# Up products of the first expert moved into the last attention pairs, and routed down products with token columns

## The reference

```python
# sixth block, T = 2048 tokens, 32 experts, top 8 (by groups), inner size 128
topk_idx, topk_w = _gate(x, gate_w, gate_bias)          # sigmoid scores, group-limited top 8
g = jnp.einsum('th,eih->eti', x, expert_gate)
u = jnp.einsum('th,eih->eti', x, expert_up)
outs = jnp.einsum('eti,ehi->eth', jax.nn.silu(g) * u, expert_down)
final = (gathered * topk_w[:, :, None]).sum(1)          # gathered: outs of the chosen experts
shared = _mlp(residuals, shared_gate, shared_up, shared_down)
x = x + final + shared
```

## Time and profile before

| | us |
|---|---|
| median of 3 runs (1290.94 to 1304.84) | 1292.93 |
| the profiled execution | 1292.72 |
| its span | 1290.9 |
| TensorE busy in the span | 1203.8 |
| VectorE, ScalarE, GpSimd busy | 805.8, 639.8, 559.0 |

### The profile page before, as it was taken

One profiled execution on the slowest core, in us unless ns is written; L12 is line 12 of the kernel. 1 busy time (PEld: TensorE's weight loads), 2 busy tenths in 40 slices (PEclk: granted clock), 3 DMA queues, 4 the chain that ended last, 5 costly groups with the idle time before them and its releaser, 6 DMA issues.

```text
span 1290.9 us, 31700 instructions
## 1 busy us (share of the span) xinstructions
PE 1203.8 (93%) x10556; PEld 985.2 (76%) x10564; DVE 805.8 (62%) x1769; ACT 639.8 (50%) x1389; POOL 559.0 (43%) x833
## 2 busy tenths in 40 slices
PE   6899999979997778998998999999999999999998
PEld 5677777757774446877776888888888888888887
DVE  4688888757776885648997776444444544444444
ACT  5766666634544886545555343433433433433333
POOL 2244444467774443548886423323323233233232
PEclk9899999989999998999998999999999999999999
DMA  8200000000000000210000133332333333333332
GB/s 283 60 18 16 16 16 8 2 1 2 0 0 33 1 0 16 68 42 2 0 1 1 44 117 116 106 110 100 114 114 110 109 133 107 114 114 103 110 99 77
DMA packets 34041, 80.13 MB, mean 62 GB/s; under 512 B 4416, under 2 KB 12096, under 8 KB 33984
## 3 DMA queue, kind: packets, MB, share of 16 engines
q1 hardware_dynamic: 32800, 78.09, 18.7%
q10 hardware_dynamic: 1184, 1.31, 0.3%
HBM read 77.03 MB, written 2.36 MB: 62 GB/s over the span
## 4 chain that ended last, share of the span: by engine, by line
PE 78%; DVE 8%; issue 5%; POOL 4%; ACT 4%; DMA 0%; DVEq 0%; POOLq 0%; ACTq 0%; SPq 0%
PE ps L2158 10%; PE ps L2160 10%; PE ps L2159 10%; PE ps L2179 5%; PE ps L2181 5%; PE ps L2180 5%; PE ps L421 4%; PE ps L968 3%; PE ps L436 3%; PE ps L409 3%; PE ps L959 2%; POOL Sm L1204 2%; PE ps L947 2%; PE ps L938 2%; PE ps L975 2%
## 5 line engine op out<-in xcount | busy, mean ns | idle before, releaser
L2417 POOL TENSOR_TENSOR sw<-sg,wb 128x512 f32<-128x512 f32 x136 | 176.9, 1301 | 392.2 <-ACT sg L2268 354.8
L2337 DVE TENSOR_TENSOR a<-sw,ps 128x512 f32<-128x512 f32 x136 | 93.5, 687 | 231.2 <-POOL sw L2417 230.9
L2273 ACT ACTIVATE ah<-a 128x512 fp32r<-128x512 f32 x136 | 86.1, 633 | 292.9 <-DVE a L2337 266.4
L2158 PE MATMUL ps<-Hh,wh 128*128 128x512 f32 x544 | 217.4, 400 | 0.3 <-issue 0.3
L2160 PE MATMUL ps<-Hh,wl 128*128 128x512 f32 x544 | 215.8, 397 | 0.0
L2159 PE MATMUL ps<-Hl,wh 128*128 128x512 f32 x544 | 215.8, 397 | 0.0
L2179 PE MATMUL ps<-wh,ah 128*128 128x256 f32 x544 | 153.8, 283 | 0.1
L2181 PE MATMUL ps<-wh,al 128*128 128x256 f32 x544 | 152.8, 281 | 0.0
L2180 PE MATMUL ps<-wl,ah 128*128 128x256 f32 x544 | 152.2, 280 | 0.0
L2341 DVE TENSOR_TENSOR al<-a,ah 128x512 fp32r<-128x512 f32 x136 | 96.3, 708 | 61.5 <-ACT ah L2273 58.1
L674 ACT ACTIVATE Pr<-ps,mx 128x256 f32<-128x256 f32 x256 | 103.9, 479 | 61.2 <-DVE mx L575 61.2
(11 more groups left out here) (227 smaller groups left out, 2443.1 us busy)
## 6 DMA issues: line engine op xcount, KB each, us to landing
wb<-token_weights SPq DMA_DIRECT2D x64, 512.0 KB, 3.6
raw<-in_ew SPq DMA_DIRECT2D x66, 384.0 KB, 3.0
cT<-in_ctxT SPq DMA_DIRECT2D x16, 256.0 KB, 2.7
cx<-in_ctxT SPq DMA_DIRECT2D x15, 256.0 KB, 2.7
X<-in_x SPq DMA_DIRECT2D x1, 1536.0 KB, 7.5
wqkv<-in_wqkv SPq DMA_DIRECT2D x2, 768.0 KB, 5.5
raw3g<-in_wg SPq DMA_DIRECT2D x1, 1024.0 KB, 5.4
raw3u<-in_wu SPq DMA_DIRECT2D x1, 1024.0 KB, 7.6
```

The source lines that it names most:

```text
L2158: eng.matmul(ps[:, bank, :], wh[:, u, w], HhT[:, c, cols], start=(c == 0), stop=False)
L2337: eng.tensor_tensor(a[:, tt, :], sw[:, tt, :], ps[:, UB[tt], :], ALU.mult).then_inc(m_a, 1)
L2417: eng.tensor_tensor(sw[:, tt, :], sg[:, tt, :], wb[:, u, tt * UT:(tt + 1) * UT], ALU.mult).then_inc(m_sw, 1)
```

## The change

1. The up products of n = 0, both halves, are issued inside body(15) of the attention: `first_up(0)` after scores(15,1), `first_up(1)` after rturn(12). The stretch by hand keeps the gate products of n = 0 alone, and those of half 1 now stand before pv(15,1).
2. The splits of the first two experts' gate and up weights move forward: first_high(0) in body(14) and first_high(1) in body(15) to just after turned(i-1,1), ahead of exps(i,0); first_low(0) in body(14) ahead of mask(14,1), first_low(1) after mask(15,1).
3. The router's first Sigmoid moves to body(15), ahead of exps(15,0). silu(0,0) moves ahead of turned(15,1).
4. From n = 4 on, down products have the down weights as stationary operand and stream 512 tokens of ah or al: 6 matmuls a half in place of 12. The sums are then transposed (256 columns x 512 tokens). `summed` copies them to SBUF (half by ScalarE, half by VectorE) and `turn_back` transposes them on TensorE in 8 transposes of 128 x 128 a half of 512 tokens, into the same banks, before `add`. This is done after n = 35 and after n = 67.
5. For n = 36 and 37 the order is written out: turn_back(0,0), gate_up(37) half 0, turn_back(0,1), down(36) half 0. The first add after n = 35 stays in VectorE's body(36), the second moves to body(37).

```diff
@@ attention, tensor body
                 scores(i, u, 1)
...
+            if closing(i) and not proj:
+                g["first_up"](eng, 0)
             if mid:
                 turn(i, u, 0)
...
                 g["route"]["turn"](eng, i - 3, v)
+            if closing(i) and not proj:
+                g["first_up"](eng, 1)
             if mid:
                 pv(i, u, 0)
@@ attention, vector body
+            elif not closing(i) and not proj:
+                g["first_low"](eng, 0)
             if tail:
                 normalise(i - 1, v)
...
                 mask(i, 1)
+            if closing(i) and not proj:
+                g["first_low"](eng, 1)
...
-            if not proj and isinstance(i, int) and i >= NPAIR - 2:
-                g["first_low"](eng, i - NPAIR + 2)
@@ attention, scalar body
                 turned(i - 1, 1)
+            if not proj and isinstance(i, int) and i >= NPAIR - 2:
+                g["first_high"](eng, i - NPAIR + 2)
+            if closing(i) and not proj:
+                g["route"]["scores"](eng, 0)
...
                 exps(i, 1)
-            if not proj and isinstance(i, int) and i >= NPAIR - 2:
-                g["first_high"](eng, i - NPAIR + 2)
@@ experts
+    def first_up(eng, tt):
+
+        if tt == 0:
+            eng.wait_ge(g["a_ve"], 8 * NPAIR)
+            eng.wait_ge(g["ln_hT"], g["lnt"][4] + NPAIR)
+        products(eng, 0, 0, tt, 0, 1)
@@ down
-            for j in range(4):
+            for m in range(0 if known(n, 4) else 2):
+                w = slice(512 + m * P, 512 + (m + 1) * P)
+                bank = ps[:, OB[tt] + m, :]
+                eng.matmul(bank, wh[:, u, w], ah[:, tt, :], start=first, stop=False)
+                eng.matmul(bank, wh[:, u, w], al[:, tt, :], start=False, stop=False)
+                ins = eng.matmul(bank, wl[:, u, w], ah[:, tt, :], start=False, stop=last)
+            for j in range(4 if known(n, 4) else 0):
...
+        def turn_back(s, tt):
+
+            eng.wait_ge(m_oa, 2 * s + tt + 1)
+            eng.wait_ge(m_od, 2 * s + tt + 1)
+            for j in range(4):
+                for m in range(2):
+                    at = DIM * (j % 2) + m * P
+                    ins = eng.transpose(ps[:, OB[tt] + j // 2, at:at + P], OT[:, tt, m, j * P:(j + 1) * P], ident[:, :])
+                if j % 2:
+                    ins.then_inc(m_tt, 1)
...
         vacated_front()
-        gate_up(0, 0, 0, 0)
+        half_up(0, 0, 0, 0, 0)
         turn(15, 1, 1)
         rturn(eng, 13, 1)
+        half_up(0, 0, 1, 0, 0)
         pv(15, 1, 1)
-        gate_up(0, 0, 1, 0)
...
-        for n in range(NE + 2, NE + 4):
-            step(n, n % 2, 1)
+        step(NE + 2, 0, 1)
+        turn_back(0, 0)
+        gate_up(NE + 3, 1, 0, 1)
+        turn_back(0, 1)
+        down(NE + 2, 0, 0)
+        gate_up(NE + 3, 1, 1, 1)
+        down(NE + 2, 0, 1)
...
+        for tt in range(2):
+            turn_back(1, tt)
@@ scalar
+        def summed(n, tt):
+
+            eng.wait_ge(m_d, given(m_d) + 2 * n - 2 + tt + 1)
+            eng.activation(OT[:, tt, 0, :], ps[:, OB[tt], :], ACT.Copy).then_inc(m_oa, 1)
...
-        route["scores"](eng, 0)
+        lg(eng, 12)
         eng.activation(warm[:, :], g["epsc"][:, :], ACT.Silu)
-        lg(eng, 12)
+        silu(0, 0)
         turned(15, 1)
-        silu(0, 0)
@@ vector, add and body
+                if group > 1 and j % 2 == 0:
+                    eng.wait_ge(m_tt, 4 * s + 2 * tt + j // 2 + 1)
...
+            if fixed == NE + 3:
+                add(NE + 2, 1)
...
+            if fixed == NE + 2:
+                summed(fixed, 1)
+                add(fixed, 0)
```

More of the change, by code:

```diff
@@ L2028, in experts @@
     sb, sem, ps, X, io, out = g["sb"], g["sem"], g["ps"], g["X"], g["io"], g["out"]
-    Hh, Hl, dram = g["Hh"], g["Hl"], g["wdram"]
+    Hh, Hl, dram, ident = g["Hh"], g["Hl"], g["wdram"], g["ident"]
     UT = 512
@@ L2048, in experts @@
     m_ah = sem(n + "ah", 3, "scalar"); m_al = sem(n + "al", 3, "vector")
-    m_y = sem(n + "y")
+    m_y = sem(n + "y"); m_oa = sem(n + "oa"); m_od = sem(n + "od"); m_tt = sem(n + "tt")
+    OT = g["self"]["Kbd"][:, :, :, :, :].rearrange("p u h b k -> p u h (b k)")
     g["m_out"] = m_out = sem(n + "out")
@@ L2090, in low_gu, with ready, products @@
                           ALU.subtract).then_inc(m_lg, 1)
+    def ready(eng, pairs):
+        eng.wait_ge(route["r_ht"], pairs)
+        eng.wait_ge(route["r_hl"], given(route["r_hl"]) + pairs)
+    def products(eng, n, u, tt, s, part):
+        if tt == 0:
+            eng.wait_ge(m_hg, weight(n) + 1)
+            eng.wait_ge(m_lg, given(m_lg) + weight(n) + 1)
+        if known(n, 3) and n != 1:
+            ready(eng, 8 * s + 4 * tt + 4)
+        cols = slice(2 * UT * s + UT * tt, 2 * UT * s + UT * (tt + 1))
+        bank, at, free, done = ((GB[tt], 0, m_sg, m_g), (UB[tt], 256, m_a, m_u))[part]
+        eng.wait_ge(free, given(free) + 2 * (n - 1) + tt + 1)
+        for c in range(HALF):
+            w = slice(at + c * P, at + (c + 1) * P)
+            eng.matmul(ps[:, bank, :], wh[:, u, w], HhT[:, c, cols], start=(c == 0), stop=False)
+            eng.matmul(ps[:, bank, :], wh[:, u, w], HlT[:, c, cols], start=False, stop=False)
+            ins = eng.matmul(ps[:, bank, :], wl[:, u, w], HhT[:, c, cols], start=False,
+                             stop=(c == 1))
+        ins.then_inc(done, 1)
+    def first_up(eng, tt):
+        if tt == 0:
+            eng.wait_ge(g["a_ve"], 8 * NPAIR)
+            eng.wait_ge(g["ln_hT"], g["lnt"][4] + NPAIR)
+        products(eng, 0, 0, tt, 0, 1)
     g["wb_ones"] = wb_ones
+    g["first_up"] = first_up
     g["first_high"] = lambda eng, c: high_gu(eng, c, c, 1)
@@ L2141, in tensor @@
     def tensor(eng):
-        def ready(pairs):
-            eng.wait_ge(route["r_ht"], pairs)
-            eng.wait_ge(route["r_hl"], given(route["r_hl"]) + pairs)
         def half_up(n, u, tt, s, part):
[L2148 to L2162, removed]
+            products(eng, n, u, tt, s, part)
         def gate_up(n, u, tt, s):
@@ L2187, in vacated_front @@
             eng.wait_ge(g["a_m"], 2 + 4 * NPAIR)
-            eng.wait_ge(g["a_ve"], 8 * NPAIR)
-            eng.wait_ge(g["ln_hT"], g["lnt"][4] + NPAIR)
         def vacated_back(tt):
@@ L2254, in tensor @@
             step(2 * j + NE + 5, 1, 1)
-        down(N - 1, 1, 0)
-        down(N - 1, 1, 1)
+        for tt in range(2):
+            down(N - 1, 1, tt)
+        for tt in range(2):
+            turn_back(1, tt)
     def scalar(eng):
@@ L2282, in body @@
             high_a(n, 0)
+            if isinstance(n, int) and n == NE + 2:
+                summed(n, 0)
             silu(n, 1)
@@ L2286, in body @@
             high_a(n, 1)
+            if isinstance(n, int) and n == NE + 2:
+                summed(n, 1)
             if isinstance(n, int) and n == NE + 3:
@@ L2324, in scalar @@
         from_sixth(eng, body)
+        summed(N, 0)
+        summed(N, 1)
     def vector(eng):
@@ L2342, in low_a, with summed @@
                               ALU.subtract).then_inc(m_al, 1)
+        def summed(n, tt):
+            eng.wait_ge(m_d, given(m_d) + 2 * n - 2 + tt + 1)
+            eng.tensor_copy(OT[:, tt, 1, :], ps[:, OB[tt] + 1, :]).then_inc(m_od, 1)
         def add(n, tt):
             group, s = GROUP.get(n, (3, 1))
-            eng.wait_ge(m_d, given(m_d) + 2 * n - 2 + tt + 1)
             if group > 1:
                 eng.wait_ge(m_y, 8 * group - 8)
+            else:
+                eng.wait_ge(m_d, given(m_d) + 2 * n - 2 + tt + 1)
             for j in range(4):
                 i = 8 * s + 4 * tt + j
+                if group > 1 and j % 2 == 0:
+                    eng.wait_ge(m_tt, 4 * s + 2 * tt + j // 2 + 1)
                 eng.tensor_tensor(X[:, i, :], ps[:, OB[tt] + j // 2, DIM * (j % 2):DIM * (j % 2 + 1)], X[:, i, :],
@@ L2361, in body @@
             low_a(n, 0)
-            if fixed in GROUP:
+            if fixed == 4:
                 add(fixed, 0)
+            if fixed == NE + 2:
+                summed(fixed, 0)
+            if fixed == NE + 3:
+                add(NE + 2, 1)
             if fixed in (5, 6, 7):
```

## The result

The changed kernel takes 1286.84 us (median of 19 runs, 1285.52 to 1293.9) against 1293.04 of the kernel before (19 runs). The ratio is 0.9957, 95% interval [0.9942, 0.9972], so 5.6 us faster (3.6 to 7.5). The forecast was 1292.5 with a range of 1288.0 to 1297.0. A gain of 0.4% is small, but the interval doesn't hold 1: with 19 runs of each kernel it can be told from none. The profiled execution of the changed kernel took 1291.0 us with a span of 1288.8.

The account below looks back on a forecast made before the run. TensorE, busy without a gap, was taken to bound the loop, and VectorE's chain to mul(1,0) the handover. Terms -2.6 + 2.1 + 2.1 - 1.8 = -0.2 us gave 1292.5 us, range 1288.0 to 1297.0.

Parts of the forecast that it names:

- Down products: Expert loop: 6 down matmuls of 512 columns for 12 of 256 save 2.6 us (1.3 to 3.8).
- 0.02 us less in each of 128 halves: Expert loop: a down half takes 1.40 us, 6 matmuls at the gate's 0.2333, instead of 1.42.
- Middle: Turning back after n = 35: transposes and a short wait add 2.1 us (1.8 to 2.7).
- The wait for adds behind low_a(37,0): In the middle: TensorE waits about 0.2 us for VectorE's moved adds, 0.6 if GpSimd slows VectorE.
- End: After the last product: a copy and all eight adds on VectorE make the end 2.1 us later (2.0 to 2.4).
- Handover: From attention to experts: four moves together bring VectorE's mul(1,0) 1.8 us earlier (-3.6 to 0).
- +0.35: Handover: Sigmoid and table loads ahead of exps(15,0) cancel the earlier mask's gain and delay it by 0.35 us.
- the lower clock from 698, as now: Handover: TensorE's clock still falls at 698, ending near 705 rather than 708.4; assumed for the -1.8 us.
- rival 1: Handover: the fill holds the clock up, front -3.6, sum -2.0, giving 1290.7 us; chance 0.20.
- The table switch of 2.66 us: ScalarE at the handover: by the skill, exps(15,0) would come 2.7 us later; the prediction used the trace instead.
- Sum: Whole kernel: loop, middle, end and handover terms add to -0.2 us, forecast 1292.5 us.
- The 2.5 ns a matmul: Expert loop: by the skill's fixed price, 6 fewer matmuls in 128 halves save an estimated 1.9 us.

Follow-up runs that it names:

- down alone: Kernel before with only the token-column down products, copies and turning back; handover as before. Ratio 0.9967 against the kernel before.
- down in pieces: Changed kernel with each 512-column down matmul made as two of 256 columns, tokens still moving. Ratio 0.9989 against the kernel before.
- up products behind: Changed kernel with the first expert's up products back behind body(15); splits and Sigmoid stay moved. Ratio 1.0006 against the kernel before.
- late-Sigmoid: Changed kernel with the router's first Sigmoid left behind body(15). Ratio 0.9956 against the kernel before.
- all in pieces: Changed kernel with down, gate and up matmuls all made as two of 256 columns. 1284.01 us, ratio 0.9913 against the kernel before.

## Why the prediction was wrong

**Down products (-2.6 forecast, -6.0 measured).** This is the step that failed: "0.02 us less in each of 128 halves", with bounds of 0.01 to 0.03 from the precision of the readings. It is the only term outside its bounds (-1.3 to -3.8). The half lost 0.0467 us, in two parts.

Gate and up, whose code does not change and which the prediction put at no change without a row, go from 2.8075 to 2.790 us. That is 0.0175 of the 0.0467, 2.2 us in 128 halves, and "down alone" shows it as well. With down in pieces they take 2.800: so 0.0075 comes with the exchanged operands of down at 256 columns, and 0.010 with its width. Matmul by matmul, as the mean of 35 halves from start to start, it lies in the first two gate matmuls behind the down products: 0.243 and 0.231 us before, 0.231 and 0.226 after. The other ten keep their times.

Down itself gave 0.029 rather than 0.02, or 3.7 us. The prediction gave its matmuls the gate's interval, 0.2333; they run at 1.390 / 6 = 0.2317.

The coarse reading is not what failed. I read 2.80 us for gate and up off one half, where the mean is 2.8075. With the mean the same sum would have been 1.419 - 2.8075 / 2 = 0.015 us a half, -2.0 us, and so further off. What was wrong is that an interval seen beside 256-column neighbours and behind the old form of down was taken for a property of the matmul's own width.

What the surplus over the columns is remains open. The runs bound it: the same 256-column width costs 1.4175 us with weights moving and 1.4026 with tokens moving, beside 256-column neighbours; 512 instead of 256 saves 0.013 in down and costs 0.053 in gate and up. That the same step in width has opposite signs for the two products is not explained by price per matmul, by price per column, or by change of width, alone or as a sum.

**Middle (+2.1 forecast).** Measured: 1018.64 - 1017.85 = 0.79 us for a block, twice, 0.08 after each for the first matmul of another form (1018.95 instead of 1018.87), and 1026.88 - 1026.58 = 0.30 of waiting with another 0.08: 2.1. The wait for adds behind low_a(37,0) was forecast at 0.2. The sum came out as forecast.

**End (+2.1 forecast).** From the start of the last gate product to the end of the span it is 13.81 us after and 11.71 before, so +2.1. The eight adds took 2.73 us and start 0.61 us after the copy of half 1 does.

**Handover (-1.8 forecast, -3.1 measured).** The steps held: mask(15,0) 4.68 us after vproj(15) instead of 6.54, exps(15,0) 9.38 instead of 9.10, which is +0.28 where I forecast +0.35, mul(0,0) and mul(0,1) awaited by TensorE (0.88 and 0.61 us). The clock was the wrong branch: I took "the lower clock from 698, as now", and it never fell in this profile. That is rival 1 with its -3.6, of which 3.1 came, and turn(15,1) started 14.87 us after vproj(15) where that branch said 14.94.

How much hangs on the fill (the up products inside body(15)) is shown by the run without it: 5.6 us of handover. Over all profiles, the three kernels without the fill (before, down alone, up products behind) each have 10.2 us at the low clock; of the ten with it eight have none and two have 3.4. One of these two, down in pieces, runs the changed kernel's code up to there at the same times within 0.01 us. So the fill makes the fall rarer and shorter and doesn't exclude it, and what decides between the two is not shown.

The table switch of 2.66 us that the Trainium skill gives (ScalarE: Activation LUTs, "What ACT_TABLE_LOAD costs") did not appear here either. Load, scores, load and Exp follow each other at 700.29, 701.59, 702.03 and 703.32, 1.29 us from the start of the second load to its Exp. So what spoke against this step by that page did not happen here; 0.9 us at logits(15) is what the step costs by the late-Sigmoid profile.

**Sum.** With the measured terms, -6.0 - 3.1 + 4.2 = -4.9 us, inside the interval of -3.6 to -7.5. Rival 1 (1290.7) kept my loop term and so was still high by 3.9 us. The profiled executions would have said -1.7: 3.1 us of theirs lie in the attention, ahead of the change.

The 2.5 ns a matmul of the Trainium skill (TensorE: Matmul & The Clock Gate, "Wait — 56ns, not 53.3ns?") gave 1.9 us for the loop. Its agreement with the kernel before is not a matter of coarse readings: the means give 2 x 0.1183 - 0.2340 = 0.0026 us. But it did not carry over. Measured surpluses over the columns are 18.9 ns at 512 (the changed kernel) and 7.4 at 256 (all in pieces: 114.1 - 106.7, gate and up), so for these fp32r products neither the size nor the independence of width shows.

## What to carry over

Where one engine is busy without a gap, its interval per instruction is the time. Do not assume that an interval read beside one kind of neighbour holds beside another, nor that the untouched instructions keep theirs: a more precise mean would not have helped here, a small run with the new form would have. Try other widths of the moving operand first: cutting gate and up products from 512 to 256 columns gave more here than turning the down product around, and needs no copies, while 128 columns made it 1801 us. A gap on TensorE ahead of long products costs twice, once as idle time and once as products at the low clock, so work moved into it can be worth several times its own length: first_up(0), 1.4 us of products, and first_up(1) behind it were worth 5.6 us here.

## What the hardware showed that I had not expected

Two fp32r matmuls of 256 columns took 0.228 us, one of 512 took 0.2325 (gate and up, 24 in 2.74 us, 12 in 2.79). 128 columns took 0.1117, nearly as long as 256 (0.114). Code that is nearly the same in all kernels reached vproj(15) anywhere from 689.08 to 696.97 us, with 23.9 and 47.8 us at the lower clock on the way, so one profile carries several us of luck.
